# A two-layer graph network on one core: the receiver's linear term of the edge messages moves into the weights of the node update

## The reference, cut to what matters

```python
h = relu(layernorm(x))
m = concatenate([h[dst], h[src]]) @ W_pre.T + b_pre          # one message per edge
mx, mn, s1, s2 = segment max, min, sum of m, sum of m * m, by dst
mean = s1 / deg;  var = s2 / deg - mean * mean;  std = sqrt(relu(var) + EPS)
agg = concatenate([mx, mn, mean, std])
scaled = concatenate([agg, agg * log(deg + 1), agg / log(deg + 1)])
x = x + (concatenate([h, scaled]) @ W_post.T + b_post) @ W_lin.T + b_lin
```

## Time and profile before

| what | value |
|---|---|
| time, median of three runs (range) | 1868.22 us (1868.07 to 1869.76) |
| span of the profiled execution | 1776.9 us (91.3 us below the median of the runs) |
| granted TensorE clock over the span | 0.950 |
| busy: TensorE, its weight loads | 86%, 72% |
| busy: VectorE, ScalarE, GpSimd | 89%, 60%, 73% |
| chain that ended last | VectorE 42%, TensorE 36%, issue 17% |

### The profile page before, as it was taken

How to read it: one execution, slowest core, us unless ns; L and a number is a source line. 1 busy time by engine, 2 the same in 40 slices (tenths; PEclk the granted TensorE clock), 3 DMA queues, 4 the chain that set the end, 5 groups by cost and what they waited for, 6 DMA issues and landing times.

```text
span 1776.9 us, 34948 instructions
## 1 busy us (share of the span) xinstructions
PE 1526.8 (86%) x8869; PEld 1275.2 (72%) x8869; DVE 1572.7 (89%) x5261; ACT 1067.4 (60%) x2368; POOL 1302.7 (73%) x1379
## 2 busy tenths in 40 slices
PE   2899999999997788888787879878787878888895
PEld 2799898998996577767675767667676667676774
DVE  5999999999996899989798979989797979899992
ACT  1899999999996455545454545545454545455541
POOL 1778777787787878877677777867786877778643
PEclk8899999999998899999999999989998999989997
DMA  2233333233325222222122221222122222222200
GB/s 75 83 101 106 95 105 104 97 106 99 102 95 142 61 68 69 69 63 63 54 71 70 70 68 52 73 70 73 48 73 71 75 70 69 66 60 75 70 18 17
DMA packets 104065, 134.10 MB, mean 75 GB/s; under 512 B 17344, under 2 KB 63577, under 8 KB 103978
## 3 DMA queue, kind: packets, MB, share of 16 engines
q1 hardware_dynamic: 85162, 98.55, 19.1%
q0 software_dynamic: 18816, 34.71, 6.7%
HBM read 98.27 MB, written 38.79 MB: 77 GB/s over the span
## 4 chain that ended last, share of the span: by engine, by line
DVE 42%; PE 36%; issue 17%; ACT 2%; POOL 1%; DMA 1%; DVEq 1%; SPq 0%; POOLq 0%; ACTq 0%
PE bank L556 10%; PE bank L565 5%; DVE runs L1204 3%; DVE runs L1189 3%; DVE part L1083 3%; DVE var L1240 3%; DVE var L1234 3%; DVE runs L1193 2%; PE bank L577 2%; PE bank L575 2%; DVE runs L1161 2%; PE bank L539 2%; PE bank L576 2%; DVE bn L1262 2%; PE bank L547 2%
## 5 line engine op out<-in xcount | busy, mean ns | idle before, releaser
L598 PE MATMUL bank<-comb_lo,agg_hi 128*128 128x384 f32 x588 | 221.7, 377 | 44.6 <-DVE nx L1092 36.5
L473 POOL DMA_INDIRECT y<-nout,oidx x196 | 212.2, 1083 | 54.6 <-issue 51.9
L460 POOL DMA_INDIRECT xs<-in_x,idx x196 | 203.1, 1036 | 65.0 <-issue 63.7
L460 POOL DMA_INDIRECT xd<-in_x,idx x196 | 185.5, 947 | 59.7 <-issue 59.4
L602 PE MATMUL bank<-comb_hi,agg_lo 128*128 128x384 f32 x588 | 209.6, 357 | 4.0 <-POOL agg_lo L400 4.0
L599 PE MATMUL bank<-comb_hi,agg_hi 128*128 128x384 f32 x588 | 209.0, 355 | 0.0
L556 PE MATMUL bank<-w_sb,nut 128*128 128x128 f32 x1568 | 203.8, 284 | 5.4 <-DVE nout L999 4.7
L377 POOL TENSOR_TENSOR runs<-nx,b_all 128x512 f32<-128x512 f32 x98 | 125.7, 1283 | 108.6 <-DVE nx L1009 107.6
L556 PEld LDWEIGHTS bank<-w_sb,nut 128*128 128x128 f32 x1568 | 185.6, 194 | 23.1 <-issue 14.2
L400 POOL TENSOR_TENSOR agg_lo<-whole,agg_hi 128x512 fp32r<-128x512 f32 x98 | 146.1, 1513 | 66.1 <-ACT agg_hi L848 66.1
L605 PE MATMUL bank<-comb_sd,agg_sd 128*128 128x384 f32 x392 | 169.9, 517 | 0.0
(11 more groups left out here) (196 smaller groups left out, 4788.3 us busy)
## 6 DMA issues: line engine op xcount, KB each, us to landing
xs<-in_x SPq DMA_DIRECT2D x98, 256.0 KB, 2.8
y<-nout SPq DMA_DIRECT2D x98, 256.0 KB, 2.8
inv<-inv_row SPq DMA_DIRECT2D x49, 256.0 KB, 4.6
attr<-in_edge_attr SPq DMA_DIRECT2D x48, 256.0 KB
keep<-keep_row SPq DMA_DIRECT2D x49, 128.0 KB, 2.7
reset<-reset_row SPq DMA_DIRECT2D x49, 128.0 KB, 3.1
lift<-lift_row SPq DMA_DIRECT2D x49, 128.0 KB, 4.0
xs<-in_x,idx POOLq DMA_INDIRECT x196
```

Of the source, the lines that this page charges most:

```text
L460: pool.indirect_dma_start(out=rows[:, s, j, :], out_offset=None, in_=x, in_offset=bass.IndirectOffsetOnAxis(ap=idx[:, s, which, j:j + 1], ...
L473: pool.indirect_dma_start(out=out, out_offset=bass.IndirectOffsetOnAxis(ap=oidx[:, c % 4, j:j + 1], axis=0), in_=eout[:, c % 2, j, :], in_ ...
L598: pe.matmul(acc[:, 0:SCALERS * P], hi, w_lo, start=(a == MX), stop=False, skip_group_check=True)
```

## The change

The three blocks of `comb` that act on max, min and mean are summed for each scaler (`part_sum`) and multiplied by the receiver's half of `W_pre`. The result, with `comb_x` added to scaler 1's block, is `comb_h`: 128x384 in place of the 128x128 `comb_x`. The receiver's rows times `comb_h` in `layer0` then bring the receiver's term to all three scalers. The matmuls into bank 4 and the three adds of VectorE go. The bias must be in before the scans: ScalarE reads bank 3, adds `b_pre_col` and writes bank 4, which the scans read; it makes the square in a second reading of bank 3. High and low parts are taken from `run_max` and `run_min`. Some waits change with it, and the instructions behind the removed adds stand in another order. The start gets thirteen small matmuls more and one transpose less.

```diff
@@ start, TensorE
+            for s in range(SCALERS):
+                for a in (MX, MN, ME):
+                    b = 1 + s * AGGS + a
+                    pe.matmul(bank[5][:, (1 + s) * P:(2 + s) * P], w_post_sb[:, b * P:(b + 1) * P], w_lin_t[:],
+                              start=(a == MX), stop=(a == ME))
...
+            pe.wait_ge(sem("part_sum_ready"), 1)
+            for s in range(SCALERS):
+                to = bank[5][:, s * P:(s + 1) * P]
+                mm = pe.matmul(to, w_pre_sb[:, 0:P], part_sum[:, s, :], start=True, stop=(s > 0))
+                if s == 0:
+                    mm = pe.matmul(to, w_post_sb[:, 0:P], w_lin_t[:], start=False, stop=True)
+            mm.then_inc(sem("comb_h_psum"), 1)
@@ layer0, TensorE
-                for h, w in ((hdt, comb_x_lo), (hdl, comb_x_hi), (hdt, comb_x_hi)):
-                    mm = pe.matmul(acc[:, 0:P], h[:, c % 2, cols], w[:], start=False, stop=(w is comb_x_hi and h is hdt),
-                                   skip_group_check=True)
+                for h, w in ((hdt, comb_h_lo), (hdl, comb_h_hi), (hdt, comb_h_hi)):
+                    mm = pe.matmul(acc[:, 0:SCALERS * P], h[:, c % 2, cols], w[:].rearrange("p s f -> p (s f)"),
+                                   start=False, stop=(w is comb_h_hi and h is hdt), skip_group_check=True)
@@ edge_step, TensorE
+                    pe.wait_ge(sem("e_hdl"), c + 1 + EU * i)
                     layer0(c, 0, i)
...
-                        pe.wait_ge(sem("e_sum"), c + EU * i)
                         pe.wait_ge(sem("e_bsq"), c + EU * i)
                     pe.matmul(bank[3][:], ws_t[:], hst[:, c % 2, :], start=True, stop=True).then_inc(sem("e_b_psum"), 1)
-                    pe.wait_ge(sem("e_hdt"), c + 1 + EU * i)
-                    if c >= 1:
-                        pe.wait_ge(sem(f"e_whole{ME}"), c + EU * i)
-                    pe.matmul(bank[4][:], wd_lo[:], hdt[:, c % 2, :], start=True, stop=False)
-                    pe.matmul(bank[4][:], wd_hi[:], hdt[:, c % 2, :], start=False, stop=False)
-                    pe.wait_ge(sem("e_hdl"), c + 1 + EU * i)
-                    pe.matmul(bank[4][:], wd_hi[:], hdl[:, c % 2, :], start=False, stop=True).then_inc(sem("e_a_psum"), 1)
@@ edge_step, ScalarE
+                    if c >= 1:
+                        act.wait_ge(sem("e_sum"), c + EU * i)
+                    act.activation(bank[4][:], bank[3][:], ACT.Identity, bias=b_pre_col[:]).then_inc(sem("e_b"), 1)
...
-                    act.activation(bsq[:, c % 2, :], bank[3][:], ACT.Square).then_inc(sem("e_bsq"), 1)
+                    act.activation(bsq[:, c % 2, :], bank[3][:], ACT.Square, bias=b_pre_col[:]).then_inc(sem("e_bsq"), 1)
@@ edge_step, VectorE
-                    dve.wait_ge(sem("e_bsq"), c + 1 + EU * i)
+                    dve.wait_ge(sem("e_b"), c + 1 + EU * i)
...
+                    if c >= 2:
+                        dve.wait_ge(sem(f"e_lo{MX}"), c - 1 + EU * i)
+                        dve.wait_ge(sem(f"e_lo{MN}"), c - 1 + EU * i)
...
-                    dve.scalar_tensor_tensor(whole[:, MX, :], bank[4][:], b_pre_col[:], run_max[:, b, :],
-                                             ALU.add, ALU.add).then_inc(sem(f"e_whole{MX}"), 1)
...
-                    dve.scalar_tensor_tensor(whole[:, MN, :], bank[4][:], b_pre_col[:], run_min[:, b, :],
-                                             ALU.add, ALU.add).then_inc(sem(f"e_whole{MN}"), 1)
-                if have:
-                    mix_plain(k, 1, i)
                 if ahead:
...
                     dve.tensor_tensor(var[:], run_sq[:, b, :], inv[:, s, :], ALU.mult).then_inc(sem("e_sq_mean"), 1)
-
+                if have:
+                    mix_plain(k, 1, i)
+                if ahead:
                     dve.wait_ge(sem("e_mean_b2"), c + 1 + EU * i)
-                    dve.scalar_tensor_tensor(mean_b[:], bank[4][:], b_pre_col[:], mean_b[:],
-                                             ALU.add, ALU.add).then_inc(sem(f"e_whole{ME}"), 1)
```

60 lines of the change are left out of this document (25 added, 35 removed).

## The result

The kernel after takes 1745.99 us (median of 4 runs, 1741.15 to 1747.71), the kernel before 1868.66 us: a ratio of 0.934, 95% interval 0.9326 to 0.9353. That is 122.7 us less; I had forecast 63 us less, 1805 us, in a range from 1774 us, so the time lies outside it.

The account below looks back on a forecast made before the run. GpSimd was taken to set the edge loop's pace at 22.2 us a chunk, plus stops at the loop's head. Loop -61, tail -5 and start +3 sum to -63 us: 1868.2 to 1805 us, range 1774 to 1842 us.

Parts of the forecast that it names:

- The runs lie 91.3 us over the span, which I leave as it is: Whole kernel: timed runs exceed the trace's 1776.9 us span by 91.3 us, kept unchanged, giving 1868.2 - 63 = 1805 us.
- that is GpSimd's own length: Edge loop: a chunk where GpSimd does not wait takes 22.2 us, its eight gathers, four scatters and four adds.
- Loop: The edge loop's 37 chunks at 22.2 us plus nine waits of 2.7 us: 845 us, 61 us less than 906.
- The adds: VectorE's list in each chunk: three adds go at 0.66 us each, 1.98 us per chunk.
- Start: Before the edge stage: the thirteen small matmuls for `comb_h` add 3 us, with ends at 0 and 5.
- Tail: Last steps, without gathers and bounded by VectorE: two or three chunks lose 2 us each, -5 us.
- ScalarE's write: ScalarE's added instruction per chunk, bank 3 to bank 4: 0.53 us, ends 0.3 and 1.2 us, costing nothing on the path.
- counts more: TensorE between tiles: no longer waiting for `hdl`, it may run into tile 1 while VectorE is held; no size given.
- Held each time: Rival, edge loop: VectorE never gets past GpSimd's two adds and waits 2.5 us each chunk; 1826 us, chance 0.26.
- The stop hidden: Rival, loop's head: VectorE needs 18.8 to 19.5 us, leads by over 7 us; 1781 us, chance 0.16.
- A ring over ScalarE and TensorE: Rival, edge chunks: mean, square, high part, relu, layer 0 in sequence take 22.5 to 23.3 us; 1845 us, chance 0.11.
- TensorE at half clock: Rival, edge loop: the clock falls below 0.80 and TensorE becomes the bound; 1900 us at 0.78, chance 0.05.

Follow-up runs that it names:

- the adds alone: Kernel before without VectorE's three adds, high and low parts taken from the scans, products into bank 4 kept: 1815.03 and 1815.76 us (0.9708, 0.9712).
- one place in ScalarE's list: Kernel before with the hidden layer's first half moved behind the mean's square and the maximum's high part: 1793.79 us (late signals), 1754.08 us (prompt).

## Why the prediction was wrong

**The step that failed** is "The runs lie 91.3 us over the span, which I leave as it is". The 91 us were not around the execution. They were, for the most part, chunks of 25.6 us in place of 23.3 us, because TensorE's signal for the hidden product came most often 2.4 or 3.9 us late. The change shortens this delay and the waits behind it, and so it touched them. On the level of the trace the sum of 63 us met 61 us; on the level of the runs it missed by 60. That it met 61 us is in part luck: terms were off in both directions, as follows.

**The pace** was wrong too, though the sum came out. I held GpSimd's own 22.2 us for the setter of the kernel before. Without its gathers nothing changed, and so the line "that is GpSimd's own length" fell: those chunks are 22.2 us long without gathers too, and GpSimd's own length, read in the kernel after, is 21.6 us. For the kernel after with prompt signals chunks were forecast at 22.2 us and came at 21.5 and 23.5; that GpSimd sets the pace in the short ones, as forecast, is likely by its rows and not tested.

**The terms, on the prompt level:**
- Loop: -61 forecast, -58.2 measured. I had the loop's head stand at 7.4 us with 2.7 us of it left to GpSimd; in truth the stop itself fell from 62.7 us in all to 25.0 us, and GpSimd's wait there to 1.8 us each. These 38 us of VectorE's are two thirds of the loop's gain. They came with the adds: the stop is 2.8 us wherever they are out, 4.5 us where they are put back into the kernel after. Why a shorter list shortens it is open.
- The adds: 3 x 0.66 us in 37 chunks are 73 us of VectorE's busy time, and it fell by 49.6 us (748.84 beside 798.48). The low parts of GpSimd, which no longer wait for an add, now meet VectorE's subtraction behind the mean: 2.59 us in the mean, where the earlier trace rows has 1.16 us, some 53 us in the loop. I had set half a microsecond a chunk for such a meeting and put it at line 1097, which takes 0.76 us.
- The held product fell from 1.70 to 1.10 us in the mean, which gives 22 us of these back.
- First turn: nothing forecast, -3.2 measured (107.19 us beside 110.37).
- Start: +3 forecast. The first chunk begins at 628.99 us, 1.5 us earlier than in the earlier trace rows. Tail: -5 forecast, -2.9 measured (127.08 us beside 129.96).
- ScalarE's write: 0.57 us from its start (990.83) to `bsq` (991.40), 0.53 forecast, and no cost with late signals; with prompt ones it is one of three candidates for 15 us that I had put at nothing. The 384 columns: 0.17 us each, 0.18 forecast.
- Two sums were off without harm: 37 x 22.2 is 821.4 and not 820.7 us, and TensorE's "+1 us per chunk at half clock" is +0.2 us if all its terms double (12 x 0.14 less 3 x 0.48).

**On the level of the runs**, the adds gave 53 us: the stop fell from 5.0 to 2.8 us, which is 20 us, and a chunk from 25.6 to 24.9 us. The rest came only when the products into bank 4 went and with them TensorE's stop for `hdl` between tiles 0 and 1: 92.4 us of waiting in the loop, 2.3 us a chunk. I had written that this "counts more" than the columns and then gave it no price. In the kernel after ScalarE starts 1.1 us behind the hidden product in the mean (0.04 to 2.7), in place of 2.7 us (0.8 to 4.1), and VectorE's wait for the square (2.6 us with the adds alone) ends. A chunk takes 23.1 us.

**The rivals.** "Held each time" had its sign, 2.7 us in three of four chunks of the profile after, but not its price; with prompt signals it is one chunk of four, and 0.8 us in two others. "The stop hidden" had its sign too, no wait of GpSimd at the loop's head in the profile after, but the chunks there are bounded elsewhere. "A ring over ScalarE and TensorE" came nearest to what bounds the kernel after with late signals: chunks of 23.1 us (22.5 to 23.3 said) and VectorE waiting 2.4 us in each for ScalarE's high part (over 2 us said). Its 1845 us was reckoned from the wrong level. "TensorE at half clock" did not come: the clock is 0.97 in the loop, up from 0.94.

## What to carry to other kernels

Hold the profiled execution's span against the timed runs before anything else. It was 2 us under them in every other profile here and 91 us in the one that mattered. When they differ so, the trace shows another execution than the one that is timed, and a sum made on it holds only for its like. A wait behind which unlike work stands in an in-order list multiplies what it costs: one place in ScalarE's list was worth 79 us where the signal was late and 18 us where it was prompt. And an engine that is busy for as long as its neighbour is tested by taking its work away, not by its share.

## What the runs showed of the hardware

- While GpSimd's indirect gathers are under way, a completion signal of TensorE can reach ScalarE 0.8 to 4.1 us behind the product's end, most often 2.4 or 3.9: in the kernel before 1.1 to 1.9 us behind the end of the eighth gather in each of 36 chunks. Behind the last gather of the same execution it was 0.04 us, as it is on the other level with the gathers too. What puts a set of runs on the one level or the other was not found.
- The node pass is not touched until the gathers begin: in the profile of the kernel before with late signals the event of TensorE's product of line 577 lies 0.01 us behind it in the first 95 of 98 chunks and 4.3 us behind it in the next (549 us), with the first gather at 541 us.
- On the level with late signals the profiles lack 36 to 43% of VectorE's semaphore events between 650 and 1650 us; with the gathers left out it is 9%, on the other level at most one event. Of VectorE's signals beside the gathers the starts of those who wait tell: ScalarE's line 821 follows VectorE's line 1175, beside the second gather, by 0.04 us on both levels.
- The stop at the loop's head follows VectorE's list: 6 to 7 us in the kernel before with prompt signals, 5.0 with late ones (6 to 7 us again without the gathers), 2.8 us in all kernels without the three adds.
- A `tensor_scalar` of 128x4 numbers with one input is held by GpSimd's adds for 2.7 us, as the form with two inputs is.
- A shorter list of VectorE's can cost elsewhere: GpSimd's low parts, freed from waiting, hold the next instruction of VectorE for 1.9 us more than its own length.
